# A Mamba block and a mixture of experts on one core: 144 expert tiles for 160, and a new order of the work around them

## What is computed

```
xz = x @ W_in.T;  xs, z = split(xz)                 # 512 channels each
xc = silu(causal_conv4(xs) + conv_b)
dt = (xc @ W_x.T)[:, :32];  a = softplus(dt @ W_dt.T + b_dt)
x1 = layernorm(2*x + (xc * a * silu(z)) @ W_out.T)
scores = sigmoid(x1 @ gate_w.T)                     # 16 experts in 4 groups
# keep 2 of the 4 groups, then the top 4 experts; weights normalised, times 2.5
y  = sum over the 4 experts of  w_e * (silu(x1 @ Wg_e.T) * (x1 @ Wu_e.T)) @ Wd_e.T
y += silu(x1 @ Ws_g.T) * (x1 @ Ws_u.T) @ Ws_d.T     # shared expert
out = layernorm(2*x1 + y)
```

## Time and profile before

| | us |
|---|---|
| median of 3 runs | 683.9 (683.61 to 684.25) |
| the profiled execution | 684.26 |
| its span, first to last instruction | 682.3 |
| TensorE busy in it | 558.4 (82%) |
| VectorE busy | 498.5 (73%) |
| ScalarE busy | 339.5 (50%) |
| GpSimd busy | 398.3 (58%) |

### The profile page before, as it was taken

How to read it: one execution, slowest core, us unless ns; L and a number is a source line. 1 busy time by engine, 2 the same in 40 slices (tenths; PEclk the granted TensorE clock), 3 DMA queues, 4 the chain that set the end, 5 groups by cost and what they waited for, 6 DMA issues and landing times.

```text
span 682.3 us, 12990 instructions
## 1 busy us (share of the span) xinstructions
PE 558.4 (82%) x3384; PEld 477.3 (70%) x3385; DVE 498.5 (73%) x1403; ACT 339.5 (50%) x574; POOL 398.3 (58%) x420
## 2 busy tenths in 40 slices
PE   2678899999899999986065979999999988994292
PEld 2455686767677777765054979999999988984271
DVE  2866798989888898885987835555555688897186
ACT  2674756455564745546043334555555545443413
POOL 2313023728375573728927777776767788888580
PEclk9988999999999999987678998999999999999596
DMA  7940001312132230224325456667746887872693
GB/s 198 313 147 31 32 32 66 107 73 101 58 108 92 82 121 35 99 66 149 117 71 168 135 188 199 219 195 229 221 131 203 266 272 230 257 225 84 215 410 114
DMA packets 73131, 103.37 MB, mean 152 GB/s; under 512 B 13836, under 2 KB 58388, under 8 KB 73080
## 3 DMA queue, kind: packets, MB, share of 16 engines
q1 hardware_dynamic: 55032, 62.87, 30.5%
q0 software_dynamic: 13824, 35.69, 14.3%
q10 hardware_dynamic: 4224, 4.19, 1.8%
HBM read 57.84 MB, written 49.05 MB: 157 GB/s over the span
## 4 chain that ended last, share of the span: by engine, by line
PE 42%; DVE 18%; issue 14%; POOL 14%; ACT 7%; DMA 4%; SPq 1%; POOLq 0%; DVEq 0%; ACTq 0%
PE psum L634 7%; POOL y_buf L566 7%; POOL x_buf L514 5%; PE psum L614 3%; PE psum L771 3%; PE psum L578 3%; PE psum L689 3%; PE psum L579 3%; PE psum L580 3%; DVE newton L1093 3%; PE psum L784 3%; PE psum L785 3%; PE psum L786 3%; PE psum L810 2%; PE psum L809 2%
## 5 line engine op out<-in xcount | busy, mean ns | idle before, releaser
L514 POOL DMA_INDIRECT x_buf<-row,row_id x128 | 127.0, 992 | 114.8 <-DVE row_id L1279 78.8
L566 POOL DMA_INDIRECT y_buf<-y_out,y_id x160 | 158.5, 991 | 58.3 <-issue 51.7
L784 PE MATMUL psum<-ew_gu_hi,t_hi 128*128 x320 | 94.5, 295 | 0.0
L785 PE MATMUL psum<-ew_gu_lo,t_hi 128*128 x320 | 91.1, 285 | 0.0
L786 PE MATMUL psum<-ew_gu_hi,t_lo 128*128 x320 | 91.0, 284 | 0.0
L506 POOL TENSOR_TENSOR m<-xc,zs 128x512 f32<-128x512 f32 x32 | 42.4, 1351 | 66.7 <-DVE shift L1158 52.1
L1105 DVE SCALAR_TENSOR_TENSOR xc<-psum,cw_taps,xc 128x511 f32<-128x511 f32 (+2 forms) x96 | 71.6, 747 | 8.1 <-ACT halo_x L871 5.9
L1426 DVE SCALAR_TENSOR_TENSOR e_act<-g_act,tiles_in,psum 128x128 f32<-128x128 f32 x160 | 45.0, 342 | 43.8 <-ACT g_act L1024 39.7
L634 PE MATMUL psum<-wout,m 128*128 128x256 f32 x256 | 59.1, 390 | 14.3 <-DVE m L1130 14.3
L634 PEld LDWEIGHTS psum<-wout,m 128*128 128x128 f32 x256 | 49.2, 195 | 24.4 <-DVE m L1130 17.7
L578 PE MATMUL psum<-x_hi,win_hi 128*128 128x512 f32 x128 | 54.9, 429 | 13.2 <-DVE x_lo L1136 12.2
(11 more groups left out here) (198 smaller groups left out, 1400.3 us busy)
## 6 DMA issues: line engine op xcount, KB each, us to landing
tiles_in<-x_buf SPq DMA_DIRECT2D x160, 144.0 KB
y_in<-y_buf SPq DMA_DIRECT2D x32, 512.0 KB, 6.1
x_buf<-pad_row SPq DMA_DIRECT2D x34, 144.0 KB
xT<-in_x_T SPq DMA_DIRECT2D x8, 512.0 KB
xtok<-in_x_tok SPq DMA_DIRECT2D x8, 512.0 KB, 3.4
out_dram<-res ACTq DMA_DIRECT2D x8, 512.0 KB, 4.8
y_buf<-y_out,y_id POOLq DMA_INDIRECT x160
raw_gu<-in_wg_T SPq DMA_DIRECT2D x16, 128.0 KB, 3.2
```

The source lines that it names most:

```text
L514: nc.gpsimd.indirect_dma_start(out=x_buf, out_offset=bass.IndirectOffsetOnAxis(ap=row_id[t % ROWS][:, b, k:k + 1], axis=0), in_=row[t % RO ...
L566: nc.gpsimd.indirect_dma_start(out=y_buf, out_offset=bass.IndirectOffsetOnAxis(ap=y_id[slot][:, i:i + 1], axis=0), in_=y_out[par][:, i, :] ...
L784: pe.matmul(o, t_hi[par][:, k, r], w_hi, start=k == 0, stop=False)
L785: pe.matmul(o, t_hi[par][:, k, r], w_lo, start=False, stop=False)
```

## The change

- `NTILES` goes from 2 x 80 to 144 (36 quads) for all tokens together, in one set of regions. The first table, made from the counts of the first 4 token tiles, lists 48 tiles that are surely full (`EARLY`); the second, made in the quads, lists the other 96, in three classes: those complete with the first 4 token tiles' rows, with the first 7, and with all.
- The last token tile loses its function `tile`: its steps are written between the first quads on each engine. Its routing (`route`, `pick`, `choose`, `place`, `send`) stands beside quads 0 to 3, the second table at quads 4 to 6.
- The weights' high and low parts are made in 12 pieces of 128x1024 in token tiles 0 to 5 (ScalarE, then VectorE). The low part stays on chip, the high part is stored to DRAM and loaded back before the quads.
- In the quads the token's weight is applied with the result (`result`: four copies of 256 columns with a scale), and row numbers and weights are copied by ScalarE (`result_rows`, eight of one column). `weigh` is one instruction. From quad 5 on (`DEEP`) the quads are one step further apart on each engine. All quads are written out, without loops. `y_out` has four buffers for quads 0 to 19, two then, and two of their own for the last two.
- The sums of the first 16 blocks stand beside quads 24 to 35, wholly on VectorE. Of the last 16 blocks, 12 wait for the results of the first 32 quads only, and for the last `gate_up`; two of these are summed wholly by TensorE; the pairs of the others go to VectorE. The last norms take 8 blocks each, and the last four blocks are normalised by VectorE and stored by SyncE.
- The reciprocal root takes 9 dependent steps instead of 11. The gate multiplies with the gate weights stationary (4 matmuls of 512 columns, a copy, 4 small transposes) instead of 16 of 32 columns; `ranks` has 5 matmuls for 14.
- Within a token tile the order is new: half of `shared_down`, the gate's transposes and `ranks` go to the start of the next tile, `residual` is two tiles behind, routing stands behind the norm.
- The prologue loads x first, then W_in in halves, splits in halves, orders constants anew, loads ScalarE's table early, and moves the shared weight's split into tile 0.

```
-    HTILES = -(-(N // HALVES * TOP // P + E) // (SUB * RING)) * SUB * RING
-    NTILES = HALVES * HTILES
+    EARLY = (HT * T * TOP - E * (P - 1)) // P // (SUB * RING) * SUB * RING
+    NTILES = -(-(N * TOP + E * (P - 1)) // P // (SUB * RING)) * SUB * RING
+    FIRST_DONE = -(-(HT * T * TOP + E * (P - 1)) // P // (SUB * RING)) * SUB * RING
+    MOST_DONE = -(-((NT - 1) * T * TOP + E * (P - 1)) // P // (SUB * RING)) * SUB * RING
...
+        PIECES_OF = [(0, 1, 2, 3), (4, 5, 6, 7), (8,), (9,), (10,), (11,)] + [()] * (NT - 6)
+        LATE_GATE, LATE_RANKS, LATE_SENDS, LATE_TABLE = 0, 3, 3, 6
+        DEEP = 5
...
+            def keep_high(i):
+                at_least(sp_, "w_high", i + 1)
...
+                sp_.dma_start(to, w_hi_now[:, :].bitcast(F32)).then_inc(s["w_stored"], 16)
...
+            def load_weights_up():
+                at_least(sp_, "w_stored", 16 * PIECES)
+                load_gu(0, GU_FREE[0])
+                at_least(sp_, "m_done", KI * NT)
+                at_least(sp_, "wx_mm", NT)
+                load_gu(GU_FREE[0], GU_FREE[1])
+                at_least(sp_, "wdt_mm", KI * NT)
+                at_least(sp_, "w_low", PIECES)
+                load_gu(GU_FREE[1], E)
...
+            results_sent(sp_, 1, BQ)
+            at_least(sp_, "gu_mm", NQ)
+            load_late(MOST_BLOCKS)
+            results_sent(sp_, 1, NQ)
+            load_late(LAST_BLOCKS)
...
-            for i in range(len(gu_parts)):
...
-                nc.gpsimd.tensor_tensor(ew_gu_lo[:, r, :, :], raw_gu[:, r, :, :], ew_gu_hi[:, r, :, :].bitcast(F32),
-                                        ALU.subtract).then_inc(s["ew_gu_low"], 1)
             send(NT - 2)
-            send(NT - 1)
...
+                if isinstance(q, int) and q == LATE_SENDS:
+                    send(NT - 1)
...
+            t = NT - 1
+            dt_out(t, range(KI))
+            shared_down(t - 2, range(2, SUB))
+            gate_turn(t - 1)
+            ranks(t - 2, t)
+            shared_up(t - 1, 0)
+            table_mm(0)
+            out_proj_by_pairs(t)
             at_least(pe, "table_done", 2)
             turn_x(0, 0)
+            shared_up(t - 1, 1)
+            ranks(t - 1, t)
+            shared_down(t - 1)
+            transposes(t)
+            gate_up(0, 0, tile_experts(0))
+            gate(t)
             turn_x(0, 1)
+            shared_up(t, 0)
+            gate_turn(t)
...
             def result(j, u):
...
+                for i in range(SUB):
+                    ins = A(y_out[out_slot(j, u)][:, i, :], psum[:, 6 + i // 2, (i % 2) * D:(i % 2 + 1) * D], ACT.Copy,
+                            scale=y_w[:, q % IDS, i:i + 1])
...
+            def result_rows(j, u):
+                q, slot, turn, par = quad(j, u)
+                y_left(act, j, u - IDS)
+                for i, e in enumerate(table_values(act, tile_e, q, E - 1)):
+                    A(y_ids[:, q % IDS, i:i + 1], tiles_in[:, slot, i, bass.ds(D + E + e, 1)], ACT.Copy)
+                    A(y_w[:, q % IDS, i:i + 1], tiles_in[:, slot, i, bass.ds(D + e, 1)], ACT.Copy)
```

More of the change, by code:

```diff
@@ L277, in sums_beside @@
[L277 to L290 removed]
+            return int((j if isinstance(j, int) else j.min_val) * RING + u >= HQ)
@@ L1070, in _ @@
+            normalize(t)
+            x1T_high(t)
+            each_quad(iteration)
+            act_high(0, NQ - 1)
+            result(0, NQ - 2)
+            result(0, NQ - 1)
+            for k in range(len(NORMS)):
                 out_norm(k)
@@ L1314, in table_out, with tile @@
                 for i, v in enumerate((tile_e, tile_at)):
-                    V.tensor_copy(v[:, h * HTILES:(h + 1) * HTILES], table_bank(h, i)).then_inc(s["table_done"], 1)
-            def tile(t, first=False, last=False, more=True):
+                    first = sum(LISTED[:h])
+                    V.tensor_copy(v[:, first:first + LISTED[h]], table_bank(h, i)).then_inc(s["table_done"], 1)
+            def tile(t, first=False, more=True):
+                softplus(t, 0)
+                if t > 1:
+                    residual(t - 2)
@@ new lines, in _ @@
+            t = NT - 1
+            first_table()
+            softplus(t, 0)
+            residual(t - 2)
+            gate_logits(t - 1)
+            table_out(0)
+            softplus(t, 1)
+            place(t - 2)
+            route(t - 1)
+            shared_act(t - 1, 0)
+            pick(t - 1)
+            norm_in(t, range(0, 1))
+            choose(t - 1)
+            norm_in(t, range(1, 2))
+            layer_norm(t)
+            shared_act(t - 1, 1)
+            at_least(dve, "w_stored", 16 * PIECES)
@@ new lines, in _, with pair, total_stats @@
+            for k in range(KD):
+                turned_low(0, 0, k)
+            place(t - 1)
+            x1T_low(t)
+            residual(t - 1)
+            each_quad(iteration)
+            norm(0)
+            def pair(b):
+                u = late_slot(b)
+                at_least(dve, f"y_in{u}", 16)
+                V.tensor_tensor(y_in[u][:, 0:2, :], y_in[u][:, 0:2, :], y_in[u][:, 2:4, :], ALU.add) \
+                 .then_inc(s["y_paired"], 1)
+            def total_stats(b, first):
+                at_least(dve, "y_total", b - SUB * HG + 2 - b % 2)
+                V.bn_stats(o_stats[:, b - first, :], sum_of(b // SUB, b % SUB)).then_inc(s["o_bn"], 1)
@@ new lines, in _ @@
+            at_least(dve, "o_ready", 1)
+            first, end = NORMS[1]
+            for n, b in enumerate(MOST_BLOCKS[2:]):
+                pair(b)
+                if n >= 3 and first + n - 3 < end:
+                    total_stats(first + n - 3, first)
+            for b in range(first + n - 2, end):
+                total_stats(b, first)
+            norm(1)
+            for b in LAST_BLOCKS:
+                pair(b)
+            at_least(dve, "o_ready", 2)
+            for b in range(*NORMS[2]):
+                total_stats(b, NORMS[2][0])
@@ L1521 @@
+            norm(2)
+            dve.wait_ge(s["o_ready"], len(NORMS))
+            first, end = NORMS[-1]
+            for b in range(ACT_NORMED, end):
+                i = b - first
+                V.tensor_scalar(res[:, b, :], sum_of(b // SUB, b % SUB), o_rstd[0][:, i:i + 1], o_shift[0][:, i:i + 1],
+                                ALU.mult, ALU.add).then_inc(s["o_done_dve"], 1)
 _ORDER = ("x_tok x_T w_in_T conv_w conv_b w_x_T w_dt_T b_dt w_out_T gate_w_T gate_bias "
```

1112 lines of the change are left out of this document (650 added, 462 removed).

## The result

The changed kernel takes 602.0 us (median of four runs, 600.7 to 605.3) beside 684.1 for the kernel before: a ratio of 0.881, 95% interval 0.877 to 0.885, clearly faster. The forecast was 581, with a range of 563 to 604. The sign and most of the size were right; 21 us of the saving did not come, and this part looks for them. The profiled execution is the longest of the four: 605.3, with a span of 603.6 against the 579.7 of the sum.

A forecast was written before the change was run, and what follows sets the result against it. TensorE was taken to bound the steady quads alone, GpSimd's sends the quads beside sums. Prologue 40.4, tiles 225.5, out_proj 6 to last send 292.3 and tail 21.5 gave span 579.7; + 2.0 - 0.4 = 581.3, forecast 581, range 563 to 604.

The forecast's parts named there:

- The second part: Prologue, after the first matmul: low-part splits leave the path to the first dt product, table load earlier; 4.7 us saved.
- Token tiles: out_proj 0 to 6: weight pieces add 4.5 us, tiles 2 to 5 save 1.3 each; 226.5 to 225.5.
- Start of the sends: After out_proj of tile 6: first x send at 36.5 us, first result at 80.1 after GpSimd waits 3.4.
- from quad 20 there are two, and TensorE follows GpSimd: Late quads: with two result buffers left from quad 20, TensorE waits for GpSimd's sends, 5.24 us a quad.
- the sum of 284 for TensorE's chain: From out_proj of tile 6: turn of quad 4 at 97, 31 quads of 5.61, then 12.6; ends before GpSimd's 292.3.
- Locks and GpSimd's pace: Quads: VectorE's 16 pair adds lengthen sends by 3.2 us in all; a y send costs 1.31.
- Tail: After the last send: 12 of 16 block loads start earlier, last four land at 11.6, then 9.9; 45.8 to 21.5 us.
- A quad's compute chain is the bound: Rival, quads: ScalarE at 5.6 and its waits, or VectorE behind late sums, gives 6.3 us a quad; 594, chance 0.18.
- No overlap: Rival: tail loads start only with the last send, +18 us, 599; or weights late in the gap stage, 592; chance 0.09.
- the whole lock: Rival, quads: each block's three VectorE adds stop the sends fully, 25 us for 3.2; 603, chance 0.05.
- better front stages: Rival: tiles 7 us and prologue 2 us better than costed, GpSimd never idle (-3.4); 569 or less, chance 0.09.
- the slower one: Rival: TensorE's granted clock falls to its low level in the quads; 724 us at 0.75 of them, chance 0.01.

The follow-up runs named there:

- the repetition: The changed kernel run again without any edit, to see its spread: 601.4 us, ratio 0.881.
- e6: Changed kernel with the second table's first VectorE steps split over quads 4 and 5, the rest in 6 and 7: 600.8 us, ratio 0.880.
- e3: Changed kernel without the 16 block loads beside quads and without their sums on VectorE: 595.1 us, ratio 0.871.
- e11: Changed kernel with eight more one-column copies a quad on ScalarE, on the slow chip: 720.6 us, ratio 0.909.
- e7: Changed kernel with two swaps in the token tiles: gate logits' reduction ahead of residual, z projection 0 ahead of shared_up 0: 592.0 us, ratio 0.866.
- e5: Changed kernel with 160 tiles in place of 144, four quads of padding more: 616.4 us, ratio 0.903.
- e10: Changed kernel with the 12 late block loads also waiting for the last result send, on the slow chip: 732.8 us, ratio 0.926.
- e2: Changed kernel with the block loads beside quads begun two quads later (lag 6 for 4): 602.0 us, ratio 0.880.

## Why the prediction was right and wrong

- **Prologue, +4.1.** The halves of the weight were costed with "about 1.0 of waits". With x loaded first the weight lands later: ScalarE waits 2.88 for it. The first matmul is at 10.91 (9.24 in the repetition) for 8:

```profile
4.56 1.06 ACT L1017 ACTIVATE x_hi<-xT 128x1024 fp32r<-128x1024 f32 x1 [2.46 <-DMA xT<-in_x_T]
8.49 1.06 ACT L1146 ACTIVATE win_hi<-sp 128x1024 fp32r<-128x1024 f32 x1 [2.88 <-DMA sp<-in_w_in_T]
9.58 1.22 DVE L1644 TENSOR_TENSOR win_lo<-sp,win_hi 128x1024 fp32r<-128x1024 f32 x1 [2.71 <-ACT win_hi L1146]
```

  In the earlier trace rows the whole weight was there at 5.63. The second part gave 3.7 of its 4.7 (first matmul to out_proj 33.6, for 37.3 before).
- **Token tiles, +2.1: right by two misses.** I had 37.4 for a later tile (38.7 - 1.3); it is 37.5, but only since the clock falls, which is luck. At full clock it is 36.0, and tile 1 with its four weight pieces 39.4. The clock of the earlier trace rows for the tiles was 0.99, and I let it stand for a new order of the same engine.
- **Start of the sends, +6.4.** The first x send of tile 5 is at +39.3 for 36.5. The first y send is at +85.2 for 80.1: GpSimd waits 5.60 for the first result, not 3.4, and quad 0's sends take 6.42 for 5.24:

```profile
311.44 1.01 POOL L616 DMA_INDIRECT x_buf<-row,row_id  x1 [8.42 <-DVE row_id L1505]
...
357.31 1.00 POOL L658 DMA_INDIRECT y_buf<-y_out,y_ids  x1 [5.60 <-ACT y_out L1197]
359.83 1.01 POOL L658 DMA_INDIRECT y_buf<-y_out,y_ids  x1 [1.52 <-issue]
```

- **From quad 20, +11.3: the step that failed** is "from quad 20 there are two, and TensorE follows GpSimd", with the sum of 284 for TensorE's chain under it. That chain came to 308.6: the turn of quad 4 stands at +101.2 for 97, the 31 steps behind it take 188.9 for 174, and from the last turn to the end are 18.6 for 12.6, with the last five quads of sends back to back again. In the 31 steps are three things. (1) A quad was put at 5.61, from the earlier trace rows; these rows are of the old order, and the change turns it over from quad 5: 5.7 to 5.84. (2) The second table's steps on VectorE stood in no term: 6.5 us over three steps of 5.61 from quad 4. The runs show that this one was hidden, as e6 gained nothing. (3) The 16 blocks beside quads were costed as a mean of 1.33 a quad on VectorE and as locks, not as transfers, and not as the one or two that a quad really has. One step waits for tiles behind two loads of 512 KB and SyncE's late wait (9.86 us); two wait for t_lo behind two sums in a row (6.98 each). With two blocks the forecast's own rates give VectorE 3.22 - 0.7 + 2 x 1.97 = 6.5 a quad, above TensorE's 5.61; the mean of 5.1 hid it. What is left when the blocks go (e3) is the pace: quad 20's sends to the end take 89.4 there, where GpSimd alone would need 16 x 5.17 = 83.
- **Locks and GpSimd's pace: right; ScalarE: not contradicted.** 2.1 us of locks for 3.2; a send is 1.29. ScalarE waits 1.2 us in each steady quad for the turned activation, so it seems to have room; the run that was to test it (e11) leaves that open.
- **Tail, +1.4: right**, and for its reason: without the overlap it is 15.7 longer (on the slow chip). Its parts miss both ways, -0.9 to the last pair add and +2.3 behind it.
- **The rivals.** "A quad's compute chain is the bound" comes nearest, at 594, and in part for its reason: not by ScalarE, but by late sums twice, and else by TensorE's own order and by loads. (It took 89.5/14 as 6.3; that is 6.4.) No overlap, the whole lock, better front stages and the slower one didn't come. The four fewer quads were put at 22.4; they are worth 23, less 7 that return as long steps.

Of the 21 us the runs account so: 6.3 for the results beside quads (e3, shown; how it parts into loads and adds is open), 4, 2 and 1 for prologue, tiles and tail (read from the profile), 6 for the start of the sends (read), some 6 for the pace behind quad 20 (5.72 for 5.24 a quad over 12 quads, worked out from e3). These are more than 21, as the profiled execution is 3 us above the median. The clock's part, 1.55 a tile, is shown by one undisturbed tile of the same kernel, and e7 agrees with it.

Of the 82 us that the change saved the runs price less: 15 for the four quads (e5), and 15.7 for the overlap in the tail (e10, on the slow chip). The sends of quad 3 begin 19 us earlier than in the kernel before (+122.3 for +141.5); this and the pair adds taken off GpSimd are priced by no run.

## What to carry to other kernels

Price moved work at its densest quad, not by its mean, and on every queue and engine that it passes: two blocks of 512 KB behind a late wait and ahead of a tile load made one step of TensorE 4 to 5 us longer, two sums in a row on VectorE made others 1.2 us longer, and one block a quad did neither. Two loads with the wait two quads later (e2), or the wait without loads (e3), left no wait for tiles. When an engine looks full, look for its one pause a period and for what stands ahead of its releaser: a swap of two steps on VectorE, together with one on TensorE, gave 9.5 us, half of it by the clock. A duration from the trace of before holds only for the order in which it was taken.

## What I had not expected of the hardware

In the later token tiles a pause of TensorE of 1.79 us in a stretch that is else dense was followed by some 3 us at a granted clock of 0.50 in 4 of 4 tiles of one execution and in 3 of 4 of another; with pauses of 0.6 to 0.8 us the clock stayed at 1.00 in all five tiles (e7). Each drop cost 1.55 us. The pause isn't all of it: in the kernel before, pauses of 1.6 us in three of the last four tiles brought a drop in only one of them, some 10 us behind the pause. On one chip of three the quads took 6.4 us and more in place of 5.75, with TensorE, ScalarE and VectorE waiting for nothing that the profile knows, while most token tiles were within 1 us of those elsewhere; the kernel before took 16% longer there. What this is stays open.
